# Attention and a second layer norm on one core: the softmax sums go to their reciprocals and back by transfers instead of by transposes

## The reference

```python
x = x + attn(_layernorm(x), wq, wk_down, wv_down, wk_up, wv_up, wo)   # 8 heads, 2 KV groups, latent 32
#   q = (x @ wq); k_lat = x @ wk_down; v_lat = x @ wv_down; k = k_lat @ wk_up; v = v_lat @ wv_up
#   scores = q k^T * scale, causal; probs = softmax(scores); y = probs v; return y @ wo
x = x + (_layernorm(_layernorm(x)) * ln_g + ln_b)                     # second layer as both kernels have it
```

## Time and profile before

| what | value |
|---|---|
| median of 3 runs | 462.14 us (461.03 to 465.08) |
| the profiled execution's own time | 460.89 us |
| its span, first to last instruction | 459.2 us |
| mean granted TensorE clock | 0.975 of full speed |
| TensorE busy | 413.5 us (90%) |
| DVE, ACT, POOL busy | 280.7, 250.5, 225.1 us (61%, 55%, 49%) |
| chain that ended last | PE 66%, DVE 11%, POOL 7%, ACT 6%, issue 6%, DMA 2% |

### The profile page before, as it was taken

One profiled execution on the slowest core, in us unless ns is written; L12 is line 12 of the kernel. 1 busy time (PEld: TensorE's weight loads), 2 busy tenths in 40 slices (PEclk: granted clock), 3 DMA queues, 4 the chain that ended last, 5 costly groups with the idle time before them and its releaser, 6 DMA issues.

```text
span 459.2 us, 6945 instructions
## 1 busy us (share of the span) xinstructions
PE 413.5 (90%) x2556; PEld 244.2 (53%) x2556; DVE 280.7 (61%) x426; ACT 250.5 (55%) x484; POOL 225.1 (49%) x186
## 2 busy tenths in 40 slices
PE   5888889999999999999999999999999998989991
PEld 3573556555655565545655565545656474533541
DVE  6256865656657466556967476553966486614546
ACT  2423337655566665655665665555745656567640
POOL 2002132366635862376635852376336945586352
PEclk9967989999999999999999999999999999999997
DMA  6684900375014601065034601065052601001011
GB/s 207 150 104 124 140 3 1 120 184 79 1 33 55 89 1 47 14 86 77 1 84 52 87 2 47 13 97 66 1 99 35 87 2 47 1 2 47 0 48 46
DMA packets 20609, 27.35 MB, mean 60 GB/s; under 512 B 2528, under 2 KB 12768, under 8 KB 20448
## 3 DMA queue, kind: packets, MB, share of 16 engines
q1 hardware_dynamic: 19712, 25.43, 30.7%
q10 hardware_dynamic: 864, 1.48, 0.9%
HBM read 6.72 MB, written 4.19 MB: 24 GB/s over the span
## 4 chain that ended last, share of the span: by engine, by line
PE 66%; DVE 11%; POOL 7%; ACT 6%; issue 6%; DMA 2%; SPq 0%; DVEq 0%; POOLq 0%; ACTq 0%
PE u_ps L565 13%; PE st_ps L519 12%; PE mx_ps L540 11%; PE sh_ps L576 7%; PE sh_ps L626 6%; PE sh_ps L670 5%; DVE mx_part L966 5%; POOL pr L1288 5%; ACT pr L800 3%; PE mx_ps L546 3%; PE sh_ps L619 2%; DMA qs<-q_lo 2%; POOL pr L1275 1%; PE sh_ps L655 1%; PE sh_ps L611 1%
## 5 line engine op out<-in xcount | busy, mean ns | idle before, releaser
L966 DVE TENSOR_REDUCE mx_part<-mx_ps 128x2 f32<-128x1024 f32 (+3 forms) x160 | 175.4, 1114 | 93.9 <-PE mx_ps L546 55.7
L800 ACT ACTIVATE pr<-st_ps 128x512 f32<-128x512 f32 (+1 forms) x304 | 166.9, 574 | 88.3 <-PE st_ps L519 78.2
L1288 POOL TENSOR_TENSOR pr<-pr 128x768 f32<-128x768 f32 (+4 forms) x60 | 144.4, 2410 | 66.5 <-PE u_ps L565 43.8
L519 PE MATMUL st_ps<-qs,ks 98*128 98x512 f32 (+1 forms) x304 | 140.1, 470 | 10.5 <-ACT pr L800 10.0
L540 PE MATMUL mx_ps<-ks,qs 96*128 96x512 f32 (+3 forms) x384 | 110.6, 369 | 5.3 <-DVE mx_part L966 3.7
L1275 POOL TENSOR_SCALAR_AFFINE_SELECT pr<-pr 128x512 f32<-128x512 f32 x64 | 40.8, 638 | 115.1 <-ACT pr L800 114.9
L519 PEld LDWEIGHTS st_ps<-qs,ks 98*128 98x128 f32 x304 | 56.9, 188 | 63.3 <-ACT pr L800 36.2
L540 PEld LDWEIGHTS mx_ps<-ks,qs 96*128 96x128 f32 x384 | 70.2, 195 | 23.6 <-DVE mx_part L966 9.6
L565 PE MATMUL u_ps<-pr,v 128*32 128x512 f32 (+3 forms) x768 | 72.3, 492 | 1.5 <-POOL pr L1275 1.5
L546 PE MATMUL mx_ps<-mask_r,ident_r 128*128 128x128 f32 (+2 forms) x176 | 46.2, 262 | 0.0
L565 PEld LDWEIGHTS u_ps<-pr,v 128*32 128x32 f32 x768 | 20.1, 109 | 36.9 <-issue 28.6
(11 more groups left out here) (109 smaller groups left out, 329.9 us busy)
## 6 DMA issues: line engine op xcount, KB each, us to landing
qs<-q_hi SPq DMA_DIRECT2D x32, 256.0 KB, 5.6
qs<-q_lo SPq DMA_DIRECT2D x16, 256.0 KB, 6.7
out_y<-y SPq DMA_DIRECT2D x7, 512.0 KB, 3.1
x<-in_x SPq DMA_DIRECT2D x3, 1024.0 KB, 7.9
ks<-k_hi SPq DMA_DIRECT2D x32, 64.0 KB, 5.3
x<-in_x SPq DMA_DIRECT2D x4, 256.0 KB, 5.6
pr<-in_wq ACTq DMA_DIRECT2D x1, 1024.0 KB, 7.6
ks<-k_lo SPq DMA_DIRECT2D x16, 64.0 KB, 5.9
```

Source lines behind the costliest of these rows:

```text
L519: nc.tensor.matmul(st_ps[n % 2][:, 0:nh * width], ks[g][0:KM, kt * P:(kt + 1) * P], qs[g][0:KM, c, h0:h0 + nh, off:CH], start=True, stop=T ...
L800: nc.scalar.activation(pr[:, slot, h0:h0 + nh, off:CH], st_ps[n % 2][:, 0:nh * width].rearrange("p (h q) -> p h q", h=nh), ACT.Exp, scale= ...
L966: nc.vector.tensor_reduce(mx_part[:, t // CT, own, h0:h0 + nh, t % CT], mx_ps[n % 2][:, 0:nh * pitch].rearrange("p (h k) -> p h k", h=nh)[ ...
L1288: last = nc.gpsimd.tensor_tensor(even, even, pr[:, 6 + (e // 2) % 2, h0:h1, off:CH], ALU.add)
```

## The change

For every chunk but the very last one of the kernel (15 of 16):

- After ACT's copy into `s_raw`, SP moves four of its partitions (one for each head, 512 sums each) to 32 partitions of 64 sums (`move_sums`; the target `s_part` is an unused corner of `k_lo`).
- DVE takes the reciprocals there, 64 on each of 32 partitions (`invert`), at the places in `RECIP_AT`.
- SP moves them back to the four partitions of `s_raw`, waits for that to land, and then copies each of the four to 32 partitions with four transfers (`spread_sums`, result `r_row`).
- DVE multiplies `r_row` with `u_raw` at the places in `DIVIDE_AT`. Both operands now lie in SBUF; before, one was `sh_ps`.
- The uses `sT0`, `sT1`, `rT0`, `rT1` go from both tables, with ACT's widening; the last chunk keeps them. The places of the other uses shift: `f2`, `f3` from (4,1), (5,1) to (6,3), (7,3); `xT2`, `xT3`, `m0` and `k0` by up to one tile; in g=1 `qb1` from (9,3) to (8,1), and `f0`, `f1` from (7,3), (8,3) to (9,3), (10,3). POOL's reciprocal square root for these follows: `RSQRT1_AT` 6 to 8, `RSQRT0_AT` (last window) 9 to 11.
- `u_raw` gets a buffer for each chunk. The mask for the matmuls is kept once and read four times by a stride of zero.

```diff
-WINDOW0 = [["", "xT0"], ["m1", "sum1"], ["sT1", "xT1"], ["rT1", ""], ["f2", "xT2"], ["f3", "m0"],
-           ["sum0", "xT3"], ["sT0", "k0"], ["rT0", ""], ["qa0", ""], ["k1", ""], ["qa1", ""]]
-WINDOW1 = [["", ""], ["m1", "sum1"], ["sT1", ""], ["rT1", ""], ["", "v"], ["sum0", "sT0"],
-           ["m0", "rT0"], ["qb0", "f0"], ["", "f1"], ["", "qb1"], ["", ""], ["", ""]]
+WINDOW0 = [["", "xT0"], ["m1", "sum1"], ["", "xT1"], ["", "xT2"], ["", ""], ["m0", ""],
+           ["sum0", "f2"], ["xT3", "f3"], ["k0", ""], ["qa0", ""], ["k1", ""], ["qa1", ""]]
+WINDOW1 = [["", ""], ["m1", "sum1"], ["", ""], ["", ""], ["", "v"], ["sum0", ""],
+           ["m0", ""], ["qb0", ""], ["qb1", ""], ["", "f0"], ["", "f1"], ["", ""]]
+RECIP_AT = [{(2, 3): 1, (7, 1): 0}, {(2, 3): 1, (6, 3): 0}]
+DIVIDE_AT = [{(5, 3): 1, (9, 1): 0}, {(5, 3): 1, (9, 1): 0}]
-RSQRT1_AT, RSQRT0_AT = 6, 9
+RSQRT1_AT, RSQRT0_AT = 8, 11
+            def move_sums(w, c, n):
+                sp.wait_ge(sh_read, n + 1)
+                if w or c:
+                    sp.wait_ge(r_ready, w * NC + c)
+                sp.dma_start(s_part[:, :], s_raw[0:P:DL, :]).then_inc(s_moved, 16)
+            def spread_sums(w, c):
+                sp.wait_ge(r_ready, w * NC + c + 1)
+                sp.dma_start(s_raw[0:P:DL, :], r_part[:, :]).then_inc(r_rows_in, 16)
+                if w or c:
+                    sp.wait_ge(u_ready, u_count(w, c))
+                sp.wait_ge(r_rows_in, 16 * (w * NC + c + 1))
+                for h in range(HG):
+                    sp.dma_start(r_row[h * DL:(h + 1) * DL, :],
+                                 s_raw[h * DL:h * DL + 1, None, :].to_broadcast([1, DL, CH])).then_inc(r_in, 16)
...
+                if w:
+                    act.wait_ge(u_ready, u_count(w - 1, c + 1))
+                nc.scalar.activation(u_raw[:, c, :], u_ps[:, :], ACT.Copy).then_inc(u_read, 1)
...
+            def invert(w, c):
+                dve.wait_ge(s_moved, 16 * (w * NC + c + 1))
+                nc.vector.reciprocal(r_part[:, :], s_part[:, :]).then_inc(r_ready, 1)
+            def divide(w, g, c):
+                dve.wait_ge(r_in, 16 * HG * (w * NC + c + 1))
                 dve.wait_ge(u_read, u_count(w, c + 1))
+                nc.vector.tensor_tensor(uT[g][:, c * CH:(c + 1) * CH], r_row[:, :], u_raw[:, c, :], ALU.mult
+                                        ).then_inc(u_ready, 1)
```

More of the change, by code:

```diff
@@ L174, in program @@
         k_hi = sb("k_hi", [P, T], R)
-        k_lo = sb("k_lo", [NKV * DL, T], R)
+        k_lo = sb("k_lo", [P, T], R)
         vT = k_hi[NKV * DL:P, :].bitcast(F)
@@ L432, in batch @@
                 put_rows(w, 1, use_no(b, 0, kind, "m1"))
+                if kind != FIRST:
+                    move_sums(w - 1, 1, use_no(b, 0, kind, "sum1"))
+                    spread_sums(w - 1, 1)
+                else:
+                    move_sums(w, 0, use_no(b, 0, kind, "sum0"))
                 put_rows(w + 1, 0, use_no(b, 0, kind, "m0"))
                 if kind == FIRST:
+                    spread_sums(w, 0)
                     sp.dma_start(lng[:, :], lng_d[None, :].to_broadcast([P, D])).then_inc(ln_in, 16)
@@ L440, in batch @@
                     put(b - 1, 0)
+                    move_sums(w, 0, use_no(b, 0, kind, "sum0"))
+                    spread_sums(w, 0)
                 if kind == LAST:
                     put_rows(w + 1, 1, use_no(b, 1, kind, "m1"))
+                    move_sums(w, 1, use_no(b, 1, kind, "sum1"))
+                    spread_sums(w, 1)
+                    move_sums(w + 1, 0, use_no(b, 1, kind, "sum0"))
                     put(b - 1, 1)
+                    spread_sums(w + 1, 0)
                     return
@@ L545, in mx @@
                             "p (h k) -> p h k", h=together)[:, :, width - P:width]
-                        last = nc.tensor.matmul(diagonals, ident_r[:, :], mask_r[:, 0:together, :], start=False, stop=True)
+                        last = nc.tensor.matmul(diagonals, ident_r[:, :],
+                                                mask_r[:, None, :].to_broadcast([P, together, P]), start=False, stop=True)
                 last.then_inc(mx_full, 1)
@@ L950, in _ @@
             batch(B - 1, LAST)
-            read("sum1", USES_ALL, 0, 0, 0)
-            read("sT1", USES_ALL + 1, 0, 0, 0)
+            read("sum1", USES_ALL, 2 * B, 0, 0)
+            read("sT1", USES_ALL + 1, 2 * B, 0, 0)
             act.wait_ge(tail_y, 2)
@@ L1182, in batch @@
                         for part in range(4):
+                            c = RECIP_AT[g].get((e, part))
+                            if c is not None and w - c >= 0:
+                                invert(w - c, c)
+                            c = DIVIDE_AT[g].get((e, part))
+                            if c is not None and w - c >= 0:
+                                divide(w - c, (g - c) % NKV, c)
                             if part == 1 and names[0]:
```

53 lines of the change are left out of this document (26 added, 27 removed).

## The result

The changed kernel takes 518.05 us (median of 4 runs, 512.65 to 522.16) where the kernel before takes 463.01 on the same chip: 1.115 times as long, 95% interval 1.103 to 1.127. The prediction was 449.

A forecast was written before the change was run, and what follows sets the result against it. TensorE's work plus its short waits was taken as the bound; -13.5 - 7.2 + 1.8 + 2.7 + 1.5 + 1.7 = -13.0 from 460.89 gave 447.9, forecast as a median of 449, range 439 to 460.

The forecast's parts named there:

- Way round by transfers: Moving sums out and reciprocals back by DMA for each chunk: fits the slack before DVE's places, so 0 us.
- the forecast's upper price, 9.5: Way back of the reciprocals: transfer, four issues and last landing take 6.0 to 9.5 us, against 10.1 at the shortest.
- the prediction's own sign of being wrong: Prediction is wrong if DVE waits for a DMA at most chunks; no size given.
- At (5,3) POOL is idle: Chunk 1's multiplication at (5,3): POOL's next addition starts only after the product at (6,1), so no meeting there.
- The first rival: Transfers landing later than DVE's place, 1.6 us overrun at each of 15 places: +24, 473 us; chance 0.06.
- No stack is in flight at these places: Argument against late landings: no stack transfer runs on the DMA engines while the sums' transfers do.
- The multiplication behind POOL: DVE's multiplication, both operands in SBUF, waits for POOL's addition at seven chunks 0: +1.5 us, between 0 and 16.8.
- rival (b): Each chunk 0's multiplication waits a whole POOL addition and TensorE feels it: +15, 464 us; half of them, 457; chance 0.12.
- Transposes: 30 groups of four transposes leave TensorE at 0.45 us each: -13.5 us, between 7.8 and 15.9.
- Where a saving meets another wait: At three places removed transposes only lengthen TensorE's wait involving POOL: 2.7 us back, between 0 and 2.7.
- Waits for the shared bank: TensorE's waits at removed or spaced uses go, -7.2 us; new close neighbours cost +1.8, between 0 and 6.
- Tail: Last window, f1 moved from (8,3) to (10,3), so the end comes later: +1.7 us, between 0 and 2.3.

The follow-up runs named there:

- wide_source: Changed kernel, each of the four last transfers copying 32 partitions to 32 instead of one to 32, so 31 of 32 rows hold sums: 483.88 us, ratio 1.043.
- nobody_waits: clear_of_pool plus one 8 KB transfer and the four spreads per chunk from constants, with no engine but SP waiting (ACT once at the end): 469.89 us, ratio 1.015.
- nobody_later: nobody_waits without the five transfers of the very first chunk: 458.53 us, ratio 0.989.
- no_way_round: Changed kernel without any transfer of sums; DVE inverts a constant and multiplies with a constant row, output not normalised: 475.68 us, ratio 1.026.
- clear_of_pool: no_way_round with the multiplication of chunk 0 one tile earlier, at (8,1) in place of (9,1): 458.37 us, ratio 0.986.
- dummy_old: only_left_out with four transposes of the identity, read by nobody, put back at the four old places of each window: 462.7 us, ratio 1.004.
- only_left_out: Kernel before without sT, rT, the widening and all transfers, other uses at old places, constant factor, both multiplication operands in SBUF: 463.43 us, ratio 1.002.
- own_rows: Changed kernel with the returning reciprocals in four partitions of their own, so ACT's copy waits for the move alone: 537.09 us, ratio 1.164.
- one_hop: Changed kernel with reciprocals sent straight from 32 partitions to all rows by eight transfers; ACT's copy waits for the move alone: 483.28 us, ratio 1.043.

## Why the prediction was wrong

The sum was 447.9; the kernel took 514 to 518. The steps, in the prediction's order:

- **Way round by transfers, 0. This is the step that failed.** "The landing of the last, 64 KB, between 1.8 and the 5.3": it was 5.9 in the median and 8.3 at the longest, since each spread reads one partition 32 times; no row of the kernel before showed such a source. The way back took 11.3 to 12.2 us at the 12 chunks where DVE waited for it. The rooms there were 5.6 to 10.7 and not 10.1 at the least, so even the forecast's upper price, 9.5, would not have fitted everywhere. That DVE waits for a DMA at most chunks was the prediction's own sign of being wrong. wide_source, with only the source changed, is 34 us faster. The move of the sums held: it landed in 1.8 us (issued at 455.29, reciprocal at 457.08), and DVE's two waits for it (10.1 us) lie in the last window, where DVE comes early. Two consequences had no price at all. ACT waits in order for the same landing ahead of its next sum, 26.7 us, and TensorE behind it for the exponentials. And "At (5,3) POOL is idle" is true of DVE's place but not of the time after a late landing: three multiplications of chunk 1 met POOL's addition of 4.53 us. The first rival, 473 with a chance of 0.06, had a late landing as its mechanism, with the price worked out for the way in; it came true on the way back, at more than its price.
- **"No stack is in flight at these places"** was false in the first batch: one late stack, 11.5 us in nobody_waits, gone in nobody_later.
- **The multiplication behind POOL, +1.5.** The mechanism was right and its size was off by a factor of ten: six of the seven chunks 0 met the addition, TensorE did wait at f0, and with the clock it is 17.3 us (no_way_round less clear_of_pool). That is just above the upper bound of 16.8 and above rival (b)'s 15; the choice near the lower end rested on "DVE has some slack", which leaves out f0.
- **Transposes, -13.5.** Their work on TensorE is about what it was priced at: in dummy_old the groups at 117.45, 119.39 and 128.36 us hold up the next instruction by 0.41, 0.36 and 0.35. But the kernel's time doesn't contain it: 463.4 without them, 462.7 with them put back. In the new order their absence is worth 4.7 to 7.6.
- **Where a saving meets another wait, +2.7 at three places.** The right mechanism, and in the old order the reason for the item above: the wait at the earlier trace rows grew from 0.69 to 1.25. Missing was the price behind a longer wait, up to ten microseconds at half clock at a time.
- **Waits for the shared bank, -7.2 and +1.8.** Those on `k_lo` (2.1 us in 2) are down to 1.7 in 1, those on `mx_lo` to 1.3, those on `q_lo` to 0.8, and that of f2 and the one of qb0 on the multiplication are gone. Of 7.8 us in these rows 3.8 are left, where the forecast left 2.4 with its new ones, so most of it came. clear_of_pool, with the new tables, is 5.1 under only_left_out; the two differ in the multiplication's place too, so how much is the tables' is not told apart.
- **Tail, +1.7.** From the end of the last exponentials to the end of the span it is 20.9 us before and 21.9 in the changed kernel and in no_way_round, so +1.0, within the bounds. The last exponentials, before and after:

```profile
437.75 0.60 ACT L800 ACTIVATE pr<-st_ps 128x512 f32<-128x512 f32 x1 [0.16 <-PE st_ps L519]
```

```profile
491.61 0.60 ACT L845 ACTIVATE pr<-st_ps 128x512 f32<-128x512 f32 x1 [1.68 <-PE st_ps L563]
```

Counted back from clear_of_pool at 458.4: 17.3 for the meeting with POOL, 8.2 for the transfers if they are fast (wide_source less no_way_round, the late stack among them), 34.2 for the slow source with all that waits for it; that is 518.1. These are differences of successive runs, so they add up by construction, and they depend on the order: the late stack alone cost 11.5 in nobody_waits, more than the 8.2 here. Of what should have been gained, the kernel before has some 4 us to give (6 by the ratio), not 13.

What stays open is how much of the 34 us is DVE's wait and how much ACT's: own_rows took ACT's away and made the landing slower at the same time, wide_source and one_hop took both away.
